# Cross-attention and feed-forward in fp32r halves: four stationary buffers for K's two-batch tiles, an earlier x of tile 1, and another order of the setup

## Chip, cores and metric

The kernel runs on one core of a Trainium2 chip. The metric is device time in microseconds, measured over whole executions; one further execution was recorded by the hardware profiler, and all rows of the trace come from it.

## What is computed

Cut to what matters:

```python
xn  = layernorm(x)                                   # (16, 1024, 512), no weights
lat = ln2(xn);  kv = ln1(ctx) @ Wkv                  # ctx (16, 64, 512), 16 heads of 64
q   = (lat @ Wq) * (1 + fside) + fside               # per batch and head
x   = x + softmax(q k^T / 8) v @ Wout
x   = x + tanh(layernorm(x) @ weight @ aux1 @ aux2 + bias)
```

Everything is float32, and products are made of a high part (fp32r) and a low part (the rest): hi x hi, hi x lo and lo x hi.

## The kernel before

x has 128 tiles of 128 rows, eight to a batch. Because the context has only 64 rows a batch, the kernel folds the weights into it: for each batch M = Wq k^T (512 x 1024, heads times context rows) and N = v Wout (1024 x 512). A tile then needs three products: scores x M into two banks, probabilities times N, and the feed-forward product with one weight W3 = weight aux1 aux2. Each of the five engines runs one program: a setup (`setup_*`), the folding of M of batches 0 and 1 (`fold_m_pe`, `m0_act`, `m0_dve`), then `slot_*` for t = 0 to 132. Slot t has the scores of tile t, the probabilities' product of tile t-2 and the feed-forward of tile t-4.

**Setup.** `steps` is one list by hand for SP, ACT, DVE and GpSimd; each engine takes out of it what concerns it, in this order, and waits on semaphores. `pe_steps` is TensorE's. "split" makes the high part (ACT, L393, L389) and the low part (DVE, L450, L445) of a weight chunk; "a12" is the evacuation of the four banks of aux1 aux2 (the mixed weight: M_hi, M_lo, L398 and L456), which w3 reads; "w3" that of W3; "stats" and "norm" are the context's layernorm on DVE; "turn" its transpose; "load" a context load. Chunk i + 5 is loaded by SP (L256) at step "split i", after low part i+1-th is done (`s_slo`), so a late low part holds SP and all that SP issues behind. `kv` steps are K and V^T products, with a store each. Beside kv 29 stands "x0", where x of tiles 0 and 1 is loaded.

**K's tiles.** From slot 2 on M of the batches 2 to 15 is made beside the main work: 128 tiles, each 128 rows of M for two (n < 32) or four batches (n >= 32). Tile n needs a stationary `wst` (both heads of Wq, 128 KB, read from `wst_scratch`, L762) and K split into `k_hi`, `k_lo` (512 columns each; a two-batch tile uses columns 0 to 255 only). `tile_pe` (L796, L797) makes four small matmuls, `tile_evacuate` (L812) copies on ACT, `tile_store` (L818) stores. The places A, B, C, D in a slot hold one tile each in slots 2 to 9. There are two buffers, `wst[n % 2]`: SP issues the load of tile n+2 when tile n+1's matmuls are done, at its place in SP's order (`next_wst`), between p's stores (L960), p's loads (L977) and others. A tile's matmuls also wait for the evacuation of the tile before, and the evacuation of tile n >= 2 waits for the store of tile n-2.

**x of a tile.** `load_xT` (L625) brings x turned into the one buffer `xT`; ACT makes `xT_hi` (L917), GpSimd `xT_lo` (L922), TensorE starts the scores (L160: passes with hi, L165: with lo) on the first and needs the second after eight matmuls. xT of tile 1 is loaded at the end of SP's setup, when the low part of tile 0 is done, and ACT splits it after exp(0) of tile 0. DVE reads the scores (L1205), takes the maximum (L1210), GpSimd subtracts it (L1333), ACT makes exp (L1110), DVE the sums (L1216), GpSimd divides (L1340), SP stores p and loads it again by columns, DVE transposes (L1223), ACT and DVE split it (L1115, L1232). The first scores are written over the buffers from which M of batch 1 is stored, so DVE waits there for these stores.

The area of 16 x 512 columns is used twice: in the setup as ring of stages, context, `ku`; later as `xr`, `S[0]`, `S[1]`, `xT`. `S[1][:, 0:D]` lies on `ctx_in[0]`, which is `ku[0]`.

Of the kernel before, what the change touches and what calls it, by code (L numbers as in the profile page):

```python
# [39 lines left out]
F32 = mybir.dt.float32  # L40
F32R = mybir.dt.float32r
ALU = mybir.AluOpType
# [3 lines left out]
P = 128  # L46
BANK = 512
EPS = 1e-5
B, ROWS, D = 16, 1024, 512
# [11 lines left out]
def build(nc, x, x_turned, ctx_rows, fs_cols, ln1_w, ln1_b, ln2_w, ln2_b, wqT, wkv, wout, ffn_wT, aux1T, aux2,  # L61
# [11 lines left out]
    with ExitStack() as ctx:  # L73
# [3 lines left out]
        def sem(name):  # L77
            return ctx.enter_context(nc.semaphore(name))
# [102 lines left out]
        for g in range(2):  # L181
# [19 lines left out]
                 ("split", 4), ("split", 5), ("split", 6), ("a12", 0), ("a12", 1), ("a12", 2), ("a12", 3),  # L201
                 ("turn", 0), ("load", 3), ("turn", 1), ("load", 4), ("stats", 2), ("norm", 2), ("split", 7), ("w3", 0),
                 ("stats", 3), ("norm", 3), ("turn", 2), ("load", 5), ("split", 8), ("w3", 1), ("split", 9),
                 ("turn", 3), ("load", 6), ("w3", 2), ("w3", 3), ("stats", 4), ("norm", 4)]
# [45 lines left out]
        def setup_sp(sp):  # L250
# [29 lines left out]
            for step, i in steps:  # L280
# [32 lines left out]
                if step == "x0":  # L313
                    sp.wait_ge(s_slo, CHUNKS)
                    load_x(sp, 0, 0)
                    load_x(sp, 1, 1)
            store_bias(12)
# [3 lines left out]
            load_xT(sp, 0)  # L321
            load_v(sp, 0)
            sp.wait_ge(s_wstw, 16 * 16)
            load_wst(sp, 0)
            load_wst(sp, 1)
# [8 lines left out]
            load_xT(sp, 1)  # L334
            load_k(sp, 0)
            store_bias(15)
# [240 lines left out]
        s_xT = sem("s_xT")  # L577
# [12 lines left out]
        s_wst, s_tw_half = two("s_wst"), two("s_tw_half")  # L590
# [32 lines left out]
        def load_xT(sp, u):  # L623
            at_least(sp, s_xTl, u)
            sp.dma_start(xT, xT_t[bass.ds(u, 1), :, :].rearrange("o p c -> (o p) c")).then_inc(s_xT, 16)  # L625
# [132 lines left out]

        def load_wst(sp, n):
            if n < TILES:  # L760
                at_least(sp, s_mt, n - 1)
                sp.dma_start(wst[n % 2][:].bitcast(F32).rearrange("p (h d) -> p h d", h=2), wst_scratch[n % 32]).then_inc(s_wst[n % 2], 16)  # L762
# [25 lines left out]
        def tile_pe(pe, n):  # L788
            nb, ps, _ = tile_bufs(n)
            pe.wait_ge(s_wst[n % 2], 16 * (n // 2) + 16)  # L790
            pe.wait_ge(s_kl, n // 4 + 1)
            at_least(pe, s_tev, n)
            for h in range(2):
                own = slice(h * nb * CTX, (h + 1) * nb * CTX)
                st = wst[n % 2][:, h * P:(h + 1) * P]
                pe.matmul(ps[:, own], st, k_hi[:, own], start=True, stop=False)  # L796
                mm = pe.matmul(ps[:, own], st, k_lo[:, own], start=False, stop=True)  # L797
            mm.then_inc(s_mt, 1)
# [113 lines left out]
        def xT_split_hi(act, u):  # L912
            act.wait_ge(s_xT, 16 * u + 16)
            if u == 0:
                act.wait_ge(s_kb, 2 * PAIRS)
            at_least(act, s_sc[1], u)
            act.copy(xT_hi[:], xT).then_inc(s_xTh, 1)  # L917

        def xT_split_lo(eng, u):
            eng.wait_ge(s_xTh, u + 1)  # L920
            at_least(eng, s_sc[1], u)
            eng.tensor_tensor(xT_lo[:], xT, xT_hi[:].bitcast(F32), ALU.subtract).then_inc(s_xTl, 1)  # L922
# [26 lines left out]
        def slot_sp(sp, t, m):  # L949
# [4 lines left out]
            def next_wst(place, u=t):  # L954
                if (u, place) in tile_at:
                    load_wst(sp, tile_at[u, place] + 2)
# [145 lines left out]
        def slot_act(act, t, m):  # L1102
# [60 lines left out]
            if t < 2:  # L1163
                ln1_stats(act, t + 1, t + 1)
            if t < T:
                exp(0)
            if t < 2:
                xT_split_hi(act, t + 1)
# [293 lines left out]
```

## Time and profile before

| | us |
|---|---|
| runs: 2064.44, 2066.11, 2069.52; median | 2066.11 |
| profiled execution, its own time | 2073.66 |
| its span | 2071.4 |
| TensorE busy | 2039.1 |
| DVE, GpSimd, ACT busy | 1515.3, 1341.8, 1319.1 |

The span is what the trace covers; the execution's time has 2.3 us around it. In a timeline row stand start, duration, engine, line, operation, output <- inputs, shapes and count; in brackets how long the engine was idle before it and who released it. SPq is the queue of SyncE, which issues the DMAs. In a row of stretches stand the stretch, its length, and each engine's busy us; then PEclk, TensorE's granted clock (1.00 is 2.4 GHz, 0.50 is 1.2 GHz; between them the stretch holds both), the busy share of the DMA engines and GB/s.

### The profile page before, as it was taken

Reading aid. Unit: us, or ns where it says so; the run is one execution under the profiler, and the core shown is the slowest. Engines: PE = TensorE matmul, PEld = TensorE weight load, DVE = VectorE, ACT = ScalarE, POOL = GpSimd, SP = SyncE. Lnnn points to the kernel's source line nnn. Section 1 sums busy time; section 2 is a strip of 40 time slices with the busy share of each in tenths; the row PEclk is TensorE's granted clock in tenths of the full one; section 3 lists DMA queues with packets and bytes.
Section 4 is the critical chain, followed back from the end, with each engine's and each line's share of the span. In section 5 each row is a group of like instructions: output and inputs, shape, how many; then the busy total and the mean of one; then the engine's idle time right before and its main releaser. Section 6 shows DMA issues by size and latency. Waiting matters only on the chain.

```text
span 2071.4 us, 31429 instructions
## 1 busy us (share of the span) xinstructions
PE 2039.1 (98%) x9232; PEld 1693.0 (82%) x9232; DVE 1515.3 (73%) x2384; ACT 1319.1 (64%) x3005; POOL 1341.8 (65%) x1463
## 2 busy tenths in 40 slices
PE   7998999999999999999999999999999999999998
PEld 6777878888888888888888888888888888888887
DVE  7566667677777777777777777777777777777776
ACT  5455566666766666666666666666666666666654
POOL 2035666766677676767677776767767676767564
PEclk9999999999999999999999999999999999999999
DMA  7556887879888787878778686878766675766653
GB/s 249 180 171 194 236 250 215 248 219 252 236 218 226 208 226 203 228 198 222 216 213 237 195 238 196 227 204 221 220 185 196 181 209 168 208 179 192 182 169 120
DMA packets 502490, 431.55 MB, mean 208 GB/s; under 512 B 54832, under 2 KB 408240, under 8 KB 502320
## 3 DMA queue, kind: packets, MB, share of 16 engines
q1 hardware_dynamic: 502320, 429.54, 74.1%
q8 instruction: 75, 1.23, 0.3%
q14 instruction: 95, 0.78, 0.1%
HBM read 251.33 MB, written 178.06 MB: 207 GB/s over the span
## 4 chain that ended last, share of the span: by engine, by line
PE 91%; DMA 3%; SPq 2%; DVE 1%; ACT 1%; issue 1%; POOL 1%; DVEq 0%; ACTq 0%; POOLq 0%
PE bank L160 37%; PE bank L1069 22%; PE bank L165 18%; PE bank L1072 11%; PE bank L797 1%; PE bank L796 1%; DMA wst<-wst_scratch 1%; DMA kv_scratch<-area 0%; DMA stage_more<-ffn_wT_dram 0%; SPq L305 0%; POOL area L1333 0%; DMA area<-x_turned_dram 0%; DMA m_scratch<-evac 0%; DMA area<-ctx_rows_dram 0%; DMA land<-m_scratch 0%
## 5 line engine op out<-in xcount | busy, mean ns | idle before, releaser
L1333 POOL TENSOR_TENSOR area<-area,row_max 128x256 f32<-128x256 f32 x512 | 354.0, 712 | 159.0 <-DVE row_max L1210 159.0
L160 PE MATMUL bank<-M_hi,xT_hi 128*128 128x512 f32 x1024 | 401.9, 393 | 3.2 <-ACT xT_hi L917 3.2
L160 PE MATMUL bank<-M_lo,xT_hi 128*128 128x512 f32 x1024 | 400.9, 392 | 0.0
L1069 PE MATMUL bank<-N_hi,pT_hi 128*128 128x512 f32 x1024 | 399.5, 390 | 1.0 <-DVE N_lo L887 0.8
L1069 PE MATMUL bank<-N_lo,pT_hi 128*128 128x512 f32 x1024 | 398.5, 389 | 0.0
L1115 ACT CAST pT_hi<-turned 128x512 fp32r<-128x512 f32 x256 | 159.1, 621 | 314.4 <-DVE turned L1223 314.4
L1340 POOL TENSOR_TENSOR area<-area,row_inv 128x512 f32<-128x512 f32 x256 | 268.8, 1050 | 111.3 <-DVE row_inv L1219 111.3
L1357 POOL TENSOR_TENSOR area<-area 128x512 f32<-128x512 f32 x127 | 166.6, 1312 | 236.2 <-ACT area L1154 236.2
L1216 DVE TENSOR_REDUCE row_sum<-area 128x8 f32<-128x512 f32 x256 | 174.3, 681 | 177.4 <-ACT area L1110 177.4
L1232 DVE TENSOR_TENSOR pT_lo<-turned,pT_hi 128x512 fp32r<-128x512 f32 x256 | 198.0, 773 | 125.0 <-ACT pT_hi L1115 124.7
L165 PE MATMUL bank<-M_hi,xT_lo 128*128 128x512 f32 x1024 | 275.5, 391 | 0.2 <-POOL xT_lo L922 0.2
L1072 PE MATMUL bank<-N_hi,pT_lo 128*128 128x512 f32 x1024 | 273.7, 389 | 0.0
L1110 ACT ACTIVATE area<-area 128x512 f32<-128x512 f32 x256 | 160.0, 626 | 137.0 <-POOL area L1333 136.7
L160 PEld LDWEIGHTS bank<-M_hi,xT_hi 128*128 128x128 f32 x1024 | 193.9, 189 | 43.5 <-ACT xT_hi L917 3.1
L165 PEld LDWEIGHTS bank<-M_hi,xT_lo 128*128 128x128 f32 x1024 | 193.4, 189 | 41.1 <-POOL xT_lo L922 0.7
L160 PEld LDWEIGHTS bank<-M_lo,xT_hi 128*128 128x128 f32 x1024 | 193.9, 189 | 39.6
L1069 PEld LDWEIGHTS bank<-N_hi,pT_hi 128*128 128x128 f32 x1024 | 192.3, 188 | 40.6 <-DVE N_lo L887 0.9
L1072 PEld LDWEIGHTS bank<-N_hi,pT_lo 128*128 128x128 f32 x1024 | 192.2, 188 | 40.0
L1069 PEld LDWEIGHTS bank<-N_lo,pT_hi 128*128 128x128 f32 x1024 | 192.3, 188 | 39.3
L1205 DVE SCALAR_TENSOR_TENSOR area<-bank,rs,area 128x512 f32<-128x512 f32 x256 | 187.6, 733 | 30.4 <-PE bank L165 26.6
L160 PE MATMUL bank<-W_hi,x2T_hi 128*128 128x512 f32 (+1 forms) x512 | 199.3, 390 | 0.0
L160 PE MATMUL bank<-W_lo,x2T_hi 128*128 128x512 f32 (+1 forms) x512 | 199.3, 390 | 0.0
(171 smaller groups left out, 3938.3 us busy)
## 6 DMA issues: line engine op xcount, KB each, us to landing
p_scratch<-area SPq DMA_DIRECT2D x256, 256.0 KB, 2.6
p_moved<-p_scratch SPq DMA_DIRECT2D x512, 128.0 KB, 4.2
area<-x_dram SPq DMA_DIRECT2D x128, 256.0 KB, 4.5
area<-x_turned_dram SPq DMA_DIRECT2D x128, 256.0 KB, 4.1
x_scratch<-area SPq DMA_DIRECT2D x127, 256.0 KB, 3.0
x_moved<-x_scratch SPq DMA_DIRECT2D x508, 64.0 KB, 3.5
y_dram<-area SPq DMA_DIRECT2D x127, 256.0 KB, 3.6
land<-m_scratch SPq DMA_DIRECT2D x120, 256.0 KB, 2.8
```

Source lines behind the costliest of these rows:

```text
L160: mm = eng.matmul(ps, sh, mv, start=(n == 0), stop=False)
L165: mm = eng.matmul(ps, sl, mh, start=False, stop=(k == len(pairs) - 1))
L1069: pe.matmul(O_ps[:], st(pT_hi, k), n_cols(mv, k), start=(k == 0 and mv is N_hi), stop=False)
L1072: mm = pe.matmul(O_ps[:], st(pT_lo, k), n_cols(N_hi, k), start=False, stop=(k == 7))
L1110: act.activation(s, s, ACT.Exp).then_inc(s_ex[q], 1)
L1115: act.copy(half_of(pT_hi, q), turned[:]).then_inc(s_pTh[q], 1)
L1205: dve.scalar_tensor_tensor(out=half_of(S[t % 2], q), in0=S_ps[q][:], scalar=rs1[:, 0:1], in1=half_of(bias, q), op0=ALU.mult, op1=ALU.add). ...
L1216: dve.tensor_reduce(row_sum[t % 2][:, hs], heads(half_of(S[t % 2], q)), AX_XY, ALU.add).then_inc(s_sum[q], 1)
L1232: dve.tensor_tensor(half_of(pT_lo, q), turned[:], half_of(pT_hi, q).bitcast(F32), ALU.subtract).then_inc(s_pTl[q], 1)
L1333: last = pool.tensor_tensor(s, s, row.to_broadcast([P, 2, 4, J2]), ALU.subtract)
L1340: pool.tensor_tensor(s, s, inv, ALU.mult).then_inc(s_p[q], 1)
L1357: pool.tensor_tensor(xr[u % RING], xr[u % RING], hid, ALU.add).then_inc(s_y, 1)
```

## The change

Three edits. In the setup, split 6 goes behind the four a12 evacuations, and w3 1 behind turn 3 and load 6. For tile 1, x is loaded right behind tile 0's into `S[1][:, 0:D]`, with a semaphore of its own, waiting for the 15th `ku` low part, and ACT splits it before exp(0) of slot 0 (for tile 2 the split stays after exp(0)); xT of tile 2 then no longer waits for tile 1's low part. For n < 32 there are four stationary buffers, the two new ones in columns 256 to 511 of `k_hi` and `k_lo`: the loads 0 and 1 are issued in "x0", 2 and 3 at the end of the setup, and at the place of tile n stands the load of n+4, which needs tile n's matmuls only.

```diff
--- before.py
+++ after.py
@@ -198,10 +198,10 @@
 
 
         steps = [("split", 0), ("split", 1), ("split", 2), ("stats", 0), ("split", 3), ("norm", 0), ("stats", 1), ("norm", 1),
-                 ("split", 4), ("split", 5), ("split", 6), ("a12", 0), ("a12", 1), ("a12", 2), ("a12", 3),
-                 ("turn", 0), ("load", 3), ("turn", 1), ("load", 4), ("stats", 2), ("norm", 2), ("split", 7), ("w3", 0),
-                 ("stats", 3), ("norm", 3), ("turn", 2), ("load", 5), ("split", 8), ("w3", 1), ("split", 9),
-                 ("turn", 3), ("load", 6), ("w3", 2), ("w3", 3), ("stats", 4), ("norm", 4)]
+                 ("split", 4), ("split", 5), ("a12", 0), ("a12", 1), ("a12", 2), ("a12", 3),
+                 ("split", 6), ("turn", 0), ("load", 3), ("turn", 1), ("load", 4), ("stats", 2), ("norm", 2), ("split", 7), ("w3", 0),
+                 ("stats", 3), ("norm", 3), ("turn", 2), ("load", 5), ("split", 8), ("split", 9),
+                 ("turn", 3), ("load", 6), ("w3", 1), ("w3", 2), ("w3", 3), ("stats", 4), ("norm", 4)]
         beside = {0: [("split", 10), ("stats", 5), ("norm", 5)], 1: [("split", 11), ("load", 7), ("stats", 6), ("norm", 6)],
                   2: [("turn", 4), ("stats", 7), ("norm", 7)], 3: [("split", 12)], 4: [("turn", 5)],
                   5: [("turn", 6), ("split", 13)], 6: [("turn", 7)],
@@ -314,15 +314,16 @@
                     sp.wait_ge(s_slo, CHUNKS)
                     load_x(sp, 0, 0)
                     load_x(sp, 1, 1)
+                    sp.wait_ge(s_wstw, 16 * 16)
+                    load_wst(sp, 0)
+                    load_wst(sp, 1)
             store_bias(12)
             for q in s_kvst:
                 sp.wait_ge(q, 16 * 16)
             load_bias(sp, 0)
             load_xT(sp, 0)
+            load_xT(sp, 1)
             load_v(sp, 0)
-            sp.wait_ge(s_wstw, 16 * 16)
-            load_wst(sp, 0)
-            load_wst(sp, 1)
             for k in range(8):
                 dc, g = m_where(2 * k)
                 for w in s_m1r:
@@ -331,8 +332,9 @@
                 if k in (2, 4):
                     store_bias(12 + k // 2)
             sp.wait_ge(s_m, 16)
-            load_xT(sp, 1)
             load_k(sp, 0)
+            load_wst(sp, 2)
+            load_wst(sp, 3)
             store_bias(15)
 
         def setup_pool(pool):
@@ -574,7 +576,7 @@
         s_xsum1, s_mean1, s_sq1, s_var1, s_rs1 = (sem(n) for n in ("s_xsum1", "s_mean1", "s_sq1", "s_var1", "s_rs1"))
         s_xsum2, s_mean2, s_sq2, s_var2, s_rs2 = (sem(n) for n in ("s_xsum2", "s_mean2", "s_sq2", "s_var2", "s_rs2"))
         s_x2w, s_x2r, s_x2t = sem("s_x2w"), sem("s_x2r"), sem("s_x2t")
-        s_xT = sem("s_xT")
+        s_xT, s_xT1 = sem("s_xT"), sem("s_xT1")
         s_xTh, s_xTl = sem("s_xTh"), sem("s_xTl")
         s_x2Th, s_x2Tl = sem("s_x2Th"), sem("s_x2Tl")
         s_sc, s_sb, s_mx, s_sub, s_ex = two("s_sc"), two("s_sb"), two("s_mx"), two("s_sub"), two("s_ex")
@@ -587,7 +589,7 @@
         s_m1r = two("s_m1r")
         s_m1w = sem("s_m1w")
         s_k0in, s_kz, s_k0h, s_k0l, s_wstw = (sem(n) for n in ("s_k0in", "s_kz", "s_k0h", "s_k0l", "s_wstw"))
-        s_wst, s_tw_half = two("s_wst"), two("s_tw_half")
+        s_wst, s_tw_half = [sem(f"s_wst{i}") for i in range(4)], two("s_tw_half")
         s_mt, s_tev, s_tw = sem("s_mt"), sem("s_tev"), sem("s_tw")
         s_land, s_lh, s_ll = sem("s_land"), sem("s_lh"), sem("s_ll")
         s_n, s_nh, s_nl = sem("s_n"), sem("s_nh"), sem("s_nl")
@@ -621,8 +623,14 @@
             sp.dma_start(xr[r], x_t[bass.ds(u, 1), :, :].rearrange("o p d -> (o p) d")).then_inc(s_xin[r], 16)
 
         def load_xT(sp, u):
-            at_least(sp, s_xTl, u)
-            sp.dma_start(xT, xT_t[bass.ds(u, 1), :, :].rearrange("o p c -> (o p) c")).then_inc(s_xT, 16)
+            if u == 1:
+                sp.wait_ge(s_kul, 2 * PAIRS - 1)
+            else:
+                at_least(sp, s_xTl, u if u > 2 else u - 1)
+            sp.dma_start(xT_in(u), xT_t[bass.ds(u, 1), :, :].rearrange("o p c -> (o p) c")).then_inc(s_xT1 if u == 1 else s_xT, 16)
+
+        def xT_in(u):
+            return S[1][:, 0:D] if u == 1 else xT
 
         def load_bias(sp, b):
             at_least(sp, s_sb[1], 8 * b)
@@ -756,10 +764,17 @@
         def first_of_pair(t):
             return [tile_at[t, place] // 4 for place in "AC" if tile_at.get((t, place), 1) % 4 == 0]
 
+        wst_bufs = [wst[0][:], wst[1][:], k_hi[:, 2 * P:4 * P], k_lo[:, 2 * P:4 * P]]
+
+        def wst_at(n):
+
+            return (n % 4, n // 4) if n < 32 else (n % 2, 8 + (n - 32) // 2)
+
         def load_wst(sp, n):
             if n < TILES:
-                at_least(sp, s_mt, n - 1)
-                sp.dma_start(wst[n % 2][:].bitcast(F32).rearrange("p (h d) -> p h d", h=2), wst_scratch[n % 32]).then_inc(s_wst[n % 2], 16)
+                at_least(sp, s_mt, n - 3 if n < 34 else n - 1)
+                i, _ = wst_at(n)
+                sp.dma_start(wst_bufs[i].bitcast(F32).rearrange("p (h d) -> p h d", h=2), wst_scratch[n % 32]).then_inc(s_wst[i], 16)
 
         def load_k(sp, kp):
             if kp < TILES // 4:
@@ -787,12 +802,13 @@
 
         def tile_pe(pe, n):
             nb, ps, _ = tile_bufs(n)
-            pe.wait_ge(s_wst[n % 2], 16 * (n // 2) + 16)
+            i, before = wst_at(n)
+            pe.wait_ge(s_wst[i], 16 * before + 16)
             pe.wait_ge(s_kl, n // 4 + 1)
             at_least(pe, s_tev, n)
             for h in range(2):
                 own = slice(h * nb * CTX, (h + 1) * nb * CTX)
-                st = wst[n % 2][:, h * P:(h + 1) * P]
+                st = wst_bufs[i][:, h * P:(h + 1) * P]
                 pe.matmul(ps[:, own], st, k_hi[:, own], start=True, stop=False)
                 mm = pe.matmul(ps[:, own], st, k_lo[:, own], start=False, stop=True)
             mm.then_inc(s_mt, 1)
@@ -910,16 +926,19 @@
             pool.tensor_tensor(rs1[:], var1[:], minus_half[:], ALU.pow).then_inc(s_rs1, 1)
 
         def xT_split_hi(act, u):
-            act.wait_ge(s_xT, 16 * u + 16)
+            if u == 1:
+                act.wait_ge(s_xT1, 16)
+            else:
+                act.wait_ge(s_xT, 16 * u if u else 16)
             if u == 0:
                 act.wait_ge(s_kb, 2 * PAIRS)
             at_least(act, s_sc[1], u)
-            act.copy(xT_hi[:], xT).then_inc(s_xTh, 1)
+            act.copy(xT_hi[:], xT_in(u)).then_inc(s_xTh, 1)
 
         def xT_split_lo(eng, u):
             eng.wait_ge(s_xTh, u + 1)
             at_least(eng, s_sc[1], u)
-            eng.tensor_tensor(xT_lo[:], xT, xT_hi[:].bitcast(F32), ALU.subtract).then_inc(s_xTl, 1)
+            eng.tensor_tensor(xT_lo[:], xT_in(u), xT_hi[:].bitcast(F32), ALU.subtract).then_inc(s_xTl, 1)
 
 
         LAST = T - 1
@@ -953,7 +972,11 @@
 
             def next_wst(place, u=t):
                 if (u, place) in tile_at:
-                    load_wst(sp, tile_at[u, place] + 2)
+                    n = tile_at[u, place]
+                    if n < 30:
+                        load_wst(sp, n + 4)
+                    elif n >= 32:
+                        load_wst(sp, n + 2)
 
             def write_p(q):
                 sp.wait_ge(s_p[q], t + 1)
@@ -1162,10 +1185,13 @@
                 v_prepare_act(act, 0)
             if t < 2:
                 ln1_stats(act, t + 1, t + 1)
+            if t == 0:
+                xT_split_hi(act, 1)
             if t < T:
                 exp(0)
+            if t == 1:
+                xT_split_hi(act, 2)
             if t < 2:
-                xT_split_hi(act, t + 1)
                 fold_n_act(act, 0, (range(3), range(3, 5))[t])
             elif t > 2:
                 evacuate("A")
```

## Rows read from the trace of the kernel before

**Rows 1.** The page: engines' busy time; x_turned loads, last figure us to landing.

```profile
PE 2039.1 (98%) x9232; PEld 1693.0 (82%) x9232; DVE 1515.3 (73%) x2384; ACT 1319.1 (64%) x3005; POOL 1341.8 (65%) x1463
...
area<-x_turned_dram SPq DMA_DIRECT2D x128, 256.0 KB, 4.1
```

**Rows 2.** Stretches: us, busy us of PE, PEld, DVE, ACT, POOL; PEclk; DMA share, GB/s.

```profile
192.10:198.30 6.20, 6.20 (x17) 5.04 (x18) 1.63 (x3) 1.71 (x4) 0.73 (x1) 0.50 0.95 251
...
210.40:215.30 4.90, 4.83 (x17) 3.90 (x18) 2.21 (x4) 3.98 (x11) 0.74 (x1) 0.67 0.90 270
...
600.00:2000.00 1400.00, 1400.00 (x6288) 1163.23 (x6287) 1055.05 (x1653) 916.97 (x2111) 978.04 (x1064) 1.00 0.75 206
```

**Rows 3.** The waits of PE: us in total, times, longest us.

```profile
PE bank L796 <- DMA wst<-wst_scratch: 7.0, 5, 2.8
...
PE bank L160 <- DVE M_lo L456: 4.0, 1, 4.0
...
PE bank L160 <- ACT xT_hi L917: 3.2, 2, 2.7
```

**Rows 4.** Timeline of DVE and SP in the setup (start, us, idle before); context landings.

```profile
21.00 1.22 DVE L450 TENSOR_TENSOR Wo_lo<-area,Wo_hi 128x1024 fp32r<-128x1024 f32 x1
...
22.13 2.48 DVE L456 TENSOR_TENSOR M_lo<-bank,M_hi 128x512 fp32r<-128x512 f32 x4
...
22.62 0.91 SPq L262 DMA_DIRECT2D area<-ctx_rows_dram  x2
...
30.42 0.68 DVE L423 BATCH_NORM_STATS2 area<-area 128x6 f32<-128x512 f32 x1
...
38.92 0.69 DVE L456 TENSOR_TENSOR W_lo<-bank,W_hi 128x512 fp32r<-128x512 f32 x1 [0.83 <-ACT W_hi L398]
...
DMA to landing us min/median/max: 4.5/5.7/9.1
```

**Rows 5.** Chain that ended last (start, us), then SP's timeline, before the first scores.

```profile
147.11 5.97 DMA area<-x_turned_dram
...
148.05 1.05 SPq L762 DMA_DIRECT2D wst<-wst_scratch  x2
```

**Rows 6.** Timeline from the first scores: DVE, POOL, PE.

```profile
160.37 0.75 DVE L1205 SCALAR_TENSOR_TENSOR area<-bank,rs,area 128x512 f32<-128x512 f32 x1 [2.00 <-DMA m_scratch<-area]
...
161.92 1.19 POOL L1333 TENSOR_TENSOR area<-area,row_max 128x256 f32<-128x256 f32 x2 [6.84 <-DVE row_max L1210]
...
164.36 1.28 POOL L922 TENSOR_TENSOR xT_lo<-area,xT_hi 128x512 fp32r<-128x512 f32 x1 [1.25 <-ACT xT_hi L917]
...
164.33 0.80 PE L160 MATMUL bank<-M_hi,xT_hi 128*128 128x512 f32 x1 [2.70 <-ACT xT_hi L917]
...
167.83 1.09 PE L165 MATMUL bank<-M_hi,xT_lo 128*128 128x512 f32 x4
```

**Rows 7.** Timeline of tile 0's turned probabilities: DVE, then PE.

```profile
178.48 0.71 DVE L1223 STREAM_TRANSPOSE turned<-p_moved 128x512 f32<-128x512 f32 x1
...
179.75 0.75 DVE L1205 SCALAR_TENSOR_TENSOR area<-bank,rs,area 128x512 f32<-128x512 f32 x1 [0.55 <-PE bank L165]
...
181.56 0.90 DVE L1232 TENSOR_TENSOR pT_lo<-turned,pT_hi 128x512 fp32r<-128x512 f32 x1 [0.34 <-ACT pT_hi L1115]
...
185.84 0.50 PE L1069 MATMUL bank<-N_hi,pT_hi 128*128 128x512 f32 x1 [0.76 <-DVE N_lo L887]
```

**Rows 8.** Timeline of ACT and PE at the tiles; landings of two evac stores (last figure).

```profile
190.60 0.37 ACT L812 COPY evac<-bank 128x256 f32<-128x256 f32 x1 [2.35 <-DMA m_scratch<-evac]
...
192.07 0.47 PE L796 MATMUL bank<-k_hi,wst 128*128 128x128 f32 x1 [2.82 <-DMA wst<-wst_scratch]
...
210.47 0.33 PE L796 MATMUL bank<-k_hi,wst 128*128 128x128 f32 x1 [2.48 <-DMA wst<-wst_scratch]
...
m_scratch<-evac SPq DMA_DIRECT2D x1, 128.0 KB, 3.0
...
m_scratch<-evac SPq DMA_DIRECT2D x1, 128.0 KB, 4.7
```

## Prediction

> **What bounds the kernel now.** I read the page first: the reader is to see TensorE busy 98% of the span [rows 1]. Then the table of stretches: from 600 to 2000 us it is busy 1400.00 of 1400.00 us at clock 1.00 [rows 2]. So nothing there can give time, and every wait that can be removed lies before 320 us. Third, the list of what TensorE waited for [rows 3]: wst loads 7.0 us in five waits, low parts of the mixed weight (M_lo, L456) 4.0, xT_hi 3.2 in two (one of them 2.7). Last, the stretches right behind the long waits [rows 2]: TensorE runs part of them at 1.2 GHz (clock 0.50) instead of 2.4. The loss is length times (1 - clock): 6.2 x 0.50 = 3.1 behind the one of 2.82, 4.9 x 0.33 = 1.6 behind the one of 2.48; behind the wait of 2.70 it is the 3.50 us from 164.33 to 167.83 [rows 6] against 1.8 at full speed, 1.7.
>
> **Part 1, order of the setup.** Today the last a12 low part ends at about 24.6: in front of the four (2.48 us) DVE does the low part of split 6, from 21.00 to 22.13 [rows 4]. With split 6 behind them DVE starts them at 21.00, ends at 23.5, and TensorE's w3 starts 1.1 us sooner. The wait of 4.0 becomes 2.9 us, more than the 2.48 behind which the clock fell, so the slow stretch stays. Little of this arrives. The context tiles go DVE-bound to turn 7, DVE is full up to its wait of 0.83 before the last w3 low part at 38.92 [rows 4], and that wait is all that it can give; w3 1, moved behind turn 3, only keeps turn 3's low part from being late for the first kv product. Against it stands SP: chunk 11 is loaded at "split 6" and waits for the seventh low part, now 24.6 instead of 22.2, and the context loads 3 and 4 are queued behind, issued at 22.62 today and at 25.1 then. With 5.7 us to landing, the median [rows 4], tile 3 comes at 30.8, where DVE wants it at 30.42: 0.3 us back. I carry 0.5 us; bounds 0 and 1.1. From kv 8 on TensorE sets the pace to 153 us and the 0.5 stays.
>
> **Part 2, SP before the first scores.** The first two wst loads cost SP 1.05 us [rows 5]. They move from behind xT(0) into the step "x0", ahead of two kv stores, the bias stores, the bias load and xT(0), in a stretch where SP issues without a pause. So xT(0) is issued 1.05 us later, less the 0.5: 0.55 late. It took 5.97 us to land (from 147.11 to 153.08), against a median of 4.1 for this transfer [rows 1, 5]; with fewer small pieces behind it, it may come up to 1.9 us sooner, or not at all sooner. I take none, since xT(1), of the same size as both wst loads, takes their place. ACT stands at xT_hi(0) with the last evacuations of M of batch 1 queued behind it, and the stores of these release DVE's first scores at 160.37 [rows 6], so that start moves to 160.9. In ends: 1.1 + 1.9 - 1.05 = 1.95 us earlier, or 1.05 later.
>
> **Part 3, x of tile 1.** TensorE comes to tile 1 at 161.63 and waits 2.70 [rows 6]. In the new kernel x is there and ACT makes xT_hi(1) before exp(0), at about 160.5. But GpSimd makes xT_lo(1) behind its two subtractions: 161.92 + 0.55 + 1.2 = 163.7, and 1.28 more is 165.0 [rows 6]. TensorE needs it 1.8 us into the tile, at about 164.0: a new wait of 1.0 where 2.7 and the slow clock were. The third pass starts at 165.0 instead of 167.83, 2.8 us earlier. Most of it is waited away again. The way of tile 0's probabilities (store, load, turn) starts from DVE's first scores, not from TensorE. What it gains is the 1.25 us that GpSimd waited for xT_hi before xT_lo [rows 6], less 0.55, and DVE's three N_lo eat half: 0.3 us at the turn of 178.48 [rows 7]. From there to the second turn, 4.0 us on, DVE waited 0.55 for TensorE's scores and 0.34 for pT_hi [rows 7]; both waits go, so the second turn comes 0.3 + 0.55 + 0.34 = 1.2 us earlier. xT(2), released one step sooner, is hidden: its cover is exp(0) of tile 1, behind which ACT makes it at about 171.6, some 1.4 us after TensorE could take it. If that cover were gone 1.4 us would go too, but only to wait at the N_lo gate (185.84 today).
>
> **Part 4, the wst buffers.** With four buffers tile 3's weight is loaded in the setup, so the wait of 2.82 at 192.07 goes. Next late is what ends it at ACT: TensorE's tile 3 waits for tile 2's evacuation, and that waited for tile 0's store until 190.60, lasting 0.37 [rows 8]. The store (issued 3.0 us before) is behind the p loads on SP, which wait for the second turn. All that is 1.2 earlier, so the evacuation ends at 190.97 - 1.2 = 189.8: the gain is 192.07 - 189.8 = 2.3 us, and TensorE stands about 2.2 us, from 187.6 (185.84 - 1.5 and the 3.3 us of its work from there). That is under 2.48, so I let the clock stay up: 3.1 more. At 210.47 the wait of 2.48 shrinks to one evacuation, 0.37 and two hand-overs, about 0.45: 2.0, and its slow stretch goes: 1.6. The other three wst waits are 7.0 - 2.82 - 2.48 = 1.7 [rows 3, 8]. Issue cost on SP in the slots is the same, one wst load at each place. From tile 32 on two buffers alternate as before: nothing.
>
> **Sum.** 2.3 + 3.1 + 2.0 + 1.6 + 1.7 = 10.7 us. Parts 1 to 3 are inside the 2.3, since the gates in a row only let the last one through. The profiled execution took 2073.66 us (span 2071.4), which gives 2063.0; it is 7.6 over the median of the runs, 2066.11. Carried over to the median: 2066.1 - 10.7 = **2055.4 us**.
>
> A price with a wide bound is that of tile 0's store: 3.0 us to land here [rows 8]; the farthest row, the evacuation's store issued near 269 us, has 4.7 [rows 8]. Then the stand of TensorE is 3.9 us and the clock falls: 2.3 - 1.7 + 0 + 2.0 + 1.6 + 1.7 = 5.9. It is nearest to the row of the same slot, so I take 3.0.
>
> **The rule that speaks against it.** In the rows the waits of 2.48, 2.70 and 2.82 us were followed by matmuls at 1.2 GHz, the wait of 0.76 was not [rows 2, 6, 7], and nothing lies between. My sum has TensorE stand 1.5, 1.0, 1.4, 1.5 and 2.2 us in the 35 us from 153 to 189, just in that gap. The Trainium skill, "TensorE: Matmul & The Clock Gate", section "A second HAM failure mode: psum-queue depth-cycling", says that frequent short idles between groups of matmuls make the clock swing too. By that rule the time would be that of rival (a) or (c). No row here shows a stand of 1 to 2.4 us, so whether the trace agrees is open.
>
> **Rivals.** (a) *Many short stands, a low clock behind each.* Five of them at 1.7 us (behind 2.70) take 8.5 off: 10.7 - 8.5 = 2.2, so 2063.9. For it: five stands close together. Against: 0.8 did nothing. 0.12. (b) *The store takes the load's place*, with its landing at 4.7 as above: gain 5.9, 2060.2. For: ACT already waited 2.35 us for that store [rows 8]. Against: fewer loads are under way there. 0.19. (c) *Slower*: the place is the same five stands; if each costs 3.1 us, as behind 192.07, they take 15.5 and the kernel ends 4.8 slower, 2070.9. It decides from 10.7 / 5 = 2.1 us a stand on. Of the three measured only one is over that. 0.03, some of it over the bound for slower. (d) *The change does not do what it says*: SP reaches the loads late all the same, because it is held by p's stores, and only the 1.7 and the 2.3 come: 4.0, 2062.1. Against: the loads of tiles 2 and 3 stand in the setup, before any store of p. 0.04.
>
> **How the numbers follow.** The forecast has 0.62. Its own range is 9 to 13 us of gain: the first scores' start may be 2.5 us earlier than taken (1.95 + 0.55), and one slow stretch kept takes 1.7. A measurement of this kernel tells 0.3% from no change, 6.2 us. Faster by more: all of the forecast and of (b), which lies at the bound, a good half and of (d) a little: 0.74. Within: (a) and the rest: 0.23. Slower: 0.03. For 8 in 10 the range must take in (b) and the good end with 2 us of scatter between runs: 2050 to 2062.5.
>
> **What would show it.** Right: no TensorE wait on wst in the list; the M_lo wait at 2.9; waits on xT_lo, xT_hi, N_lo and the evacuation of 1 to 2 us each between 153 and 190; clock 1.00 from 168 on; all starts after 320 us earlier by about 11. Wrong: slow clock behind those waits; the evacuation wait over 2.48; or xT_hi(0) over 2 us late.

## The result: 5.6 us sooner, where 10.7 were forecast

| | before | changed |
|---|---|---|
| median of 9 runs each, us | 2067.43 | 2061.85 |
| lowest, highest | 2063.59, 2070.06 | 2058.58, 2067.94 |
| profiled execution, its span | 2073.66, 2071.4 | 2061.87, 2059.7 |

The ratio is 0.9974, with a 95% interval from 0.9962 to 0.9986: 5.6 us less, just inside the 6.2 us that were called no change. The forecast's 2055.4 is some 6 us too fast, and its range up to 2062.5 holds the time. The two profiled executions alone differ by 11.8 us, which looks like the forecast. The one of before isn't among the nine runs, and is slower than all of them. That it isn't typical is half of this case.

The page of the changed kernel, engines' busy time, answers to [rows 1]:

```profile
span 2059.7 us, 31428 instructions
...
PE 2031.9 (99%) x9232; PEld 1687.4 (82%) x9232; DVE 1515.1 (74%) x2384; ACT 1318.5 (64%) x3005; POOL 1343.5 (65%) x1463
```

The waits of PE in the changed kernel (us in total, times, longest), against [rows 3]:

```profile
PE bank L812 <- ACT evac L828: 4.4, 3, 2.0
PE bank L160 <- DVE N_lo L458: 2.2, 1, 2.2
PE bank L160 <- DVE M_lo L458: 2.1, 1, 2.1
PE bank L160 <- ACT xT_hi L936: 1.9, 2, 1.1
PE bank L165 <- POOL xT_lo L941: 1.0, 1, 1.0
PE bank L546 <- DVE area L438: 0.9, 1, 0.9
```

No wait for wst is left. In the place of its 7.0 us stand 4.4 us for ACT's evacuation; the M_lo wait is 2.1 where it was 4.0. TensorE's timeline shows where the new stands are (in brackets how long it stood, and who released it):

```profile
23.45 0.47 PE L160 MATMUL bank<-M_hi 128*128 128x512 f32 x1 [2.11 <-DVE M_lo L458]
...
152.23 0.47 PE L160 MATMUL bank<-M_hi,xT_hi 128*128 128x512 f32 x1 [1.10 <-ACT xT_hi L936]
...
163.04 1.20 PE L165 MATMUL bank<-M_hi,xT_lo 128*128 128x512 f32 x4 [1.05 <-POOL xT_lo L941]
...
169.83 0.50 PE L160 MATMUL bank<-M_hi,xT_hi 128*128 128x512 f32 x1 [0.82 <-ACT xT_hi L936]
...
181.81 0.50 PE L1092 MATMUL bank<-N_hi,pT_hi 128*128 128x512 f32 x1 [0.76 <-DVE N_lo L903]
...
187.20 0.30 PE L812 MATMUL bank<-k_hi,k_lo 128*128 128x128 f32 x1 [1.97 <-ACT evac L828]
...
200.94 0.30 PE L812 MATMUL bank<-k_hi,k_lo 128*128 128x128 f32 x1 [0.84 <-ACT evac L828]
...
273.60 0.30 PE L812 MATMUL bank<-k_hi,wst 128*128 128x128 f32 x1 [1.57 <-ACT evac L828]
```

Tile 3 starts at 187.20, where it was 192.07 [rows 8], and tile 7 at 200.94, where it was 210.47. The stretches of the changed kernel behind the stand of 1.97, and in the steady part:

```profile
187.00:193.00 6.00, 5.80 (x28) 4.92 (x29) 3.53 (x5) 2.40 (x6) 1.53 (x3) 1.00 0.96 285
...
600.00:2000.00 1400.00, 1400.00 (x6287) 1163.08 (x6286) 1055.79 (x1654) 915.64 (x2107) 979.58 (x1065) 1.00 0.74 206
```

The clock is 1.00 in both, where the first was 0.50 behind 192.07 [rows 2]. The steady part is as before. Nearly all that differs lies ahead of 320 us; between 340 and 600 TensorE is idle 0.83 us, where it was 0.25. One slow stretch is left in the changed kernel, in the setup behind the N_lo stand of 2.18 at 62.90; the row gives its clock as 0.67:

```profile
62.00:66.00 4.00, 3.10 (x8) 2.48 (x9) 3.78 (x8) 0.70 (x2) 0.00 (x0) 0.67 0.41 156
```

### The profile page after: what moved, and what is told of

Its sections match the earlier page's. It is cut to its first block, busy times and chain, and to the rows that moved or that the text cites. A ratio compares the mean times of both kernels' runs of the same rounds, so it can differ in the third digit from the quotient of the medians.

```text
span 2059.7 us, 31428 instructions
## 1 busy us (share of the span) xinstructions
PE 2031.9 (99%) x9232; PEld 1687.4 (82%) x9232; DVE 1515.1 (74%) x2384; ACT 1318.5 (64%) x3005; POOL 1343.5 (65%) x1463
## 4 chain that ended last, share of the span: by engine, by line
PE 83%; DMA 2%; issue 2%; ACT 2%; DVE 2%; POOL 1%; SPq 1%; DVEq 0%; ACTq 0%; POOLq 0%
PE bank L160 33%; PE bank L1092 21%; PE bank L165 17%; PE bank L1095 10%; DMA m_scratch<-evac 2%; PE bank L813 1%; PE bank L812 1%; POOL area L1359 1%; POOL area L1366 1%; DVE area L1231 0%; DVE N_lo L903 0%; DVE row_max L1236 0%; ACT evac L828 0%; ACT bank L908 0%; DMA area<-x_turned_dram 0%
## 5 line engine op out<-in xcount | busy, mean ns | idle before, releaser
L1138 ACT CAST pT_hi<-turned 128x512 fp32r<-128x512 f32 x256 | 159.1, 622 | 317.4 <-DVE turned L1249 317.4
```

The costliest lines, as they stand in the source:

```text
L1138: act.copy(half_of(pT_hi, q), turned[:]).then_inc(s_pTh[q], 1)
```

## The experiments

Two theories were set against each other. *Profile:* the single profile of before held stands and slow stretches of its own, and terms were sized on these. *New waits:* the expected gain arrives, and waits that come in its place eat it. The first eight kernels ran in two groups of four, the last three together; each group was timed beside the kernel before, whose medians were 2067.17, 2067.73 and 2068.21.

**The kernel before once more** (no edit).

> The kernel before, unchanged, once more with a profile of its own. The changed kernel's profiled span is 11.7 us shorter than that of before (2059.7 against 2071.4), but its median only 5.6 us lower. Theory A: the profiled execution of before lies at the slow end of its own spread, because TensorE's clock fell to 1.2 GHz behind more of its waits than in most executions; then most executions here have a mean clock of 0.996 to 0.998 instead of 0.994, a span of 2062 to 2068, and the new profile shows full clock behind at least one of the waits of 2.4 to 2.8 us, with the waits themselves within 0.5 us. Theory B: the waits themselves differ from run to run, through the landings of the transfers; then the clock stays at 0.994 and the waits of 2.8 (wst), 2.7 (xT_hi) and 4.0 (M_lo) differ by over 1 us in sum. Ratio 1.000 either way.

2067.31 us, ratio 1.0002 (0.9992 to 1.0011), profiled span 2068.8, clock 0.995. Its waits of PE, then two rows of its timeline:

```profile
PE bank L160 <- DVE M_lo L456: 4.1, 1, 4.1
...
PE bank L160 <- ACT xT_hi L917: 3.9, 2, 3.4
...
PE bank L796 <- DMA wst<-wst_scratch: 3.3, 2, 2.7
```

```profile
208.16 0.30 PE L796 MATMUL bank<-k_hi,wst 128*128 128x128 f32 x1 [0.55 <-DMA wst<-wst_scratch]
...
281.86 0.30 PE L796 MATMUL bank<-k_hi,wst 128*128 128x128 f32 x1 [2.53 <-ACT evac L812]
```

The wst waits are 3.3 us in two, not 7.0 in five. Tile 7 stands 0.55 where [rows 8] had 2.48, with nothing slow behind it, and at 281.86 us there is a stand of 2.53, while the profile of before has four of 0.18 to 0.86 between 274 and 305 us. The stands of 4.0, 2.70 and 2.82 are there again (4.14, 3.42, 2.75), each with its slow clock. What made tile 7's stand is one landing of its weight, the step that ended last there, in the profile of before and then in this one:

```profile
205.66 4.77 DMA wst<-wst_scratch
```

```profile
205.28 2.76 DMA wst<-wst_scratch
```

With the setup alone the same load took 2.79 us, and the median of this transfer in the profile of before is 2.7. So this stand came of the landing, as the expectation's second theory says. Its first, full clock behind a wait of nearly the same length, is seen too, at the N_lo wait near 64 us: 2.40 us with 1.2 GHz behind it in the profile of before, 1.91 with clock 1.00 behind it here.

**The setup's order alone.** The diff is the first hunk, with nothing else changed.

> Only the order of the setup (split 6 behind a12, w3 1 behind turn 3). Theory of the prediction: w3 starts 1.1 us sooner, kv 8 only 0.5 us sooner, the rest as before: 0.5 us. Rival from the changed kernel's trace, where the wait on M_lo is 2.1 us and the clock stays up behind it: 2 us less at w3 0 and about 1.5 us at kv 8 (62.9 instead of 64.3), and this stays to the end: 1 to 2 us.

2066.53 us, 0.9996 (0.9988 to 1.0005). The M_lo stand is 3.41, and then the clock falls; DVE's first scores start at 159.1, and tile 3 comes 31.7 us behind them, as before (192.07 - 160.37).

**x of tile 1 alone** (xT(1) into `S[1][:, 0:D]`, with its semaphore and place, and the split ahead of exp(0)).

> Only x of tile 1 (loaded behind that of tile 0 into S[1], split before exp(0)). Theory of the prediction: tile 1 starts without a wait on xT_hi, waits 1 us for xT_lo, the clock stays up, and most is waited away again at the N_lo gate and at wst of tile 3, whose load stands behind p's store: 0 to 2 us at the end. Rival: the 2.8 us gained at tile 1 and its clock come through: 3 us or more.

2067.43 us, 0.9997 (0.9988 to 1.0006). The stand of 2.70 is gone, and tile 3 stands 2.65 for wst, slow clock behind it. Yet in this profile tile 3 starts 28.8 us behind DVE's first scores, where it was 31.7, so part of the gain comes through that gate. Behind it 1.2 GHz follows three stands (2.65, 1.47, 1.80). The median shows no gain; where it is lost, one profile doesn't show.

**The wst buffers alone** (`wst_bufs`, `wst_at`, the loads and their waits).

> Only the four wst buffers and their loads. Theory of the prediction: the waits of 2.8 and 2.5 us on wst become waits on the evacuation of about 2 and 0.5 us, the first loads cost SP 1.05 us before xT(0), and the gain is 6 to 9 us against the profiled execution of before, half of it slow clock. Rival: in a median execution that slow clock is mostly absent, or the evacuation wait is as long as the load's was: 2 to 4 us.

2064.01 us, 0.9982 (0.9973 to 0.9991): of the three parts alone the only one whose interval lies under 1. TensorE's timeline at tile 3, then the stretch behind it:

```profile
188.16 0.30 PE L806 MATMUL bank<-k_hi,k_lo 128*128 128x128 f32 x1 [1.81 <-ACT evac L822]
```

```profile
188.00:194.00 6.00, 5.83 (x21) 4.74 (x22) 2.85 (x4) 2.35 (x6) 0.73 (x1) 0.72 0.95 271
```

The evacuation's stand, 1.81 us where 2.2 were forecast, is followed by 1.2 GHz here: 6.0 x 0.28 = 1.7 us. The gain of 3.2 us in the median is what the expectation gave its rival, 2 to 4 us.

**The changed kernel once more** (no edit).

> The changed kernel once more, unchanged, with a profile of its own. Theory (the clock is a draw): before, 33 runs had a mean clock of 0.9965, the changed one 0.9983 in 9. Each stand of 1.8 to 2.2 us is followed by 1.2 GHz in some executions and not in others (1.97 us without in the changed kernel's profile, 1.81 and 1.93 us with it in the one with the wst buffers alone). Then the clock of 11 more runs is spread over 0.996 to 0.999, the median is 2061 to 2063, and the profile shows the same stands within 0.5 us but another set of slow stretches, each costing about 1.7 us or a multiple. Rival: the clock is a property of the kernel, 0.998 or 0.999 in all runs, and the profile repeats the one slow stretch, at the stand of 2.2 us near 63.

2062.68 us, 0.9972 (0.9958 to 0.9985), clock 0.998. Its timeline at tile 3 and the stretch behind:

```profile
189.19 0.30 PE L812 MATMUL bank<-k_hi,k_lo 128*128 128x128 f32 x1 [1.85 <-ACT evac L828]
```

```profile
189.00:195.00 6.00, 5.81 (x21) 4.72 (x22) 2.85 (x4) 2.38 (x6) 0.74 (x1) 0.72 0.95 268
```

The same kernel, the same stand within 0.12 us, and this time the clock falls. What that costs can be read directly, from tile 3's start to the first matmul of the next tile, in the first profile and in this one:

```profile
193.18 0.22 PE L812 MATMUL bank<-k_hi,wst 128*128 128x128 f32 x1
```

```profile
196.79 0.22 PE L812 MATMUL bank<-k_hi,wst 128*128 128x128 f32 x1
```

193.18 - 187.20 = 5.98 us and 196.79 - 189.19 = 7.60 us: 1.6 us, near the 1.7 by the clock. Not all of it stays. Tile 7 then stands 0.55 and not 0.84, and from tile 3's start to tile 7's the difference is 1.3 us (15.07 against 13.74). DVE's first scores start at 160.9, in the other profile at 159.0.

**A third evacuation buffer**, in the raw K's unused half, for the tiles 0 to 26, so that no evacuation waits for the store of two tiles before.

```diff
+            if nb == 2:
+                return nb, tile_ps[:, at:at + nb * P], (evac[:, 0:2 * P], evac[:, 2 * P:4 * P], k_raw[:, 2 * P:4 * P])[evac_at(n)[0]]
             return nb, tile_ps[:, at:at + nb * P], evac[:, at:at + nb * P]
+
+        def evac_at(n):
+            return (n % 3, n // 3) if n < 27 else ((n - 27) % 2, 9 + (n - 27) // 2)
...
-                at_least(act, s_tw_half[n % 2], 16 * (n // 2))
+                at_least(act, s_tw_half[evac_at(n)[0]], 16 * evac_at(n)[1])
```

> The changed kernel with a third buffer for the evacuated two-batch tiles, in the half of k_raw that they leave free, so that tile n's evacuation waits for the store of tile n-3 and not n-2 (tiles 0 to 26). Theory (the store took the load's place): the stand of 1.97 us at tile 3 shrinks to about 0.5, the one of 0.84 at tile 7 to about 0.45, and the kernel is 1.5 to 2 us faster, more where the clock fell behind that stand. The stand of 1.57 near 274, where ACT is held by the landing of a part of M and not by a store, stays. Rival: the tile waits for something else next, p or k_lo, and nothing is gained.

2060.89 us, 0.9967 (0.9957 to 0.9977). TensorE's timeline at tile 3:

```profile
185.03 0.30 PE L822 MATMUL bank<-k_hi,k_lo 128*128 128x128 f32 x1 [0.55 <-ACT k_raw L838]
```

The store was the gate: with another buffer the stand is 0.55. But in slot 8 TensorE now stands 2.64 (at 272.29), slow clock behind it. The time isn't told apart from that of the changed kernel.

**The first two wst loads back behind xT(0), xT(1) and v.**

```diff
-                    sp.wait_ge(s_wstw, 16 * 16)
-                    load_wst(sp, 0)
-                    load_wst(sp, 1)
...
             load_v(sp, 0)
+            sp.wait_ge(s_wstw, 16 * 16)
+            load_wst(sp, 0)
+            load_wst(sp, 1)
```

> The changed kernel with the first two wst loads back behind xT(0), xT(1) and v. Theory of the prediction, part 2: xT(0) is issued 1.05 us sooner, the stand before the first scores (1.10 us) falls to about 0.1, the first scores of DVE come up to 1 us sooner, and so does all that follows: 0.5 to 1 us. Rival: xT(0) then lands later, with more small pieces around it, and nothing is gained.

2062.15 us, 0.9974 (0.9965 to 0.9983). Its timeline of PE at tile 1:

```profile
160.63 0.47 PE L160 MATMUL bank<-M_hi,xT_hi 128*128 128x512 f32 x1 [1.13 <-DVE area L1231]
```

The stand for xT_hi(0) is gone, and one of the same length, for DVE's first scores, has its place. But the repeat of the changed kernel has no stand for xT_hi(0) either, so this can't be put down to the edit. DVE's first scores start at 159.7, between the two of the changed kernel. SP issues xT(0) at 145.47, and in the changed kernel's first profile at 145.63: only 0.16 of the 1.05 us show, and the 0.5 to 1 us expected in the time don't come.

**GpSimd makes xT_lo(1) ahead of its first subtraction.**

```diff
+            if t == 0:
+                xT_split_lo(pool, 1)
             if t < T:
                 subtract_maximum(0)
-            if t == 0:
-                xT_split_lo(pool, 1)
```

> The changed kernel with xT_lo(1) ahead of GpSimd's first subtraction in slot 0. Theory of the prediction, part 3: the stand of 1.05 us at tile 1 goes, but the subtraction and all of tile 0's probabilities come up to 1 us later, and since their way sets the later gates (N_lo, the evacuation), the kernel gets no faster or up to 1 us slower. Rival: TensorE's own work sets the pace there and 1 us is gained.

2061.27 us, 0.9974 (0.9964 to 0.9983). Its timeline at tile 2:

```profile
169.37 0.50 PE L160 MATMUL bank<-M_hi,xT_hi 128*128 128x512 f32 x1 [1.80 <-ACT xT_hi L936]
```

The stand of 1.05 is gone and tile 2's is 1.80 instead of 0.82: 1.05 given up, 0.98 taken back. Tile 3's is 1.77, at clock 1.00 behind it.

**The third buffer, and in slot 8 ACT's high part of the landed M behind exp(0) and the evacuation.** The slot's stand is ACT's: in the changed kernel it stood for the landing of a part of M before it came to the evacuation. ACT's timeline there:

```profile
272.04 0.62 ACT L873 CAST M_hi<-land 128x512 fp32r<-128x512 f32 x1 [3.82 <-DMA land<-m_scratch]
...
273.10 0.35 ACT L828 COPY evac<-bank 128x256 f32<-128x256 f32 x1
```

```diff
-            if t > 1 and landed_in(t) is not None:
+            if t > 1 and t != TPB and landed_in(t) is not None:
                 land_hi(act, landed_in(t))
...
                 evacuate("A")
+                if t == TPB:
+                    land_hi(act, t)
```

> The kernel with three evacuation buffers, and in slot 8 ACT takes the landed part of M after exp(0) and the evacuation of place A, not before them. Theory: the stand of 1.57 us (2.64 with three buffers) near 272 is ACT standing 3.8 to 5.3 us at that part's landing with exp(0) and the evacuation queued behind it; with the order turned the evacuation is done 1 to 3 us sooner, the stand falls below 0.6 and the kernel gains 1 to 2 us. Rival: the stand moves to exp(1) and the evacuation of place B, since GpSimd still stands for the same part ahead of its second subtraction, and nothing is gained.

2058.68 us in 5 runs, 0.9947 (0.9935 to 0.9960). ACT's timeline in it:

```profile
268.29 0.63 ACT L1143 ACTIVATE area<-area 128x512 f32<-128x512 f32 x1 [1.52 <-POOL area L1371]
...
268.83 0.35 ACT L838 COPY evac<-bank 128x256 f32<-128x256 f32 x1
...
269.73 0.62 ACT L883 CAST M_hi<-land 128x512 fp32r<-128x512 f32 x1 [0.55 <-DMA land<-m_scratch]
```

The evacuation now comes ahead of the wait, and no stand of TensorE is left in the slots 7 to 9. With 9.5 us under the kernel before (2068.21) it is the fastest version here, on few runs. Its interval ends at 0.9960; those of the changed kernel begin at 0.9962 and, in the repeat, at 0.9958, and that of the third buffer alone at 0.9957.

**The changed kernel without x of tile 1** (the second and third part only).

> The changed kernel without the part on x of tile 1 (order of the setup and wst buffers kept). Alone, that part moved nothing (ratio 0.9997). If the parts add up, this is as fast as the changed kernel, 2062 to 2063. If it only pays where the wst gate behind it is gone, this is 1 to 2 us slower than the changed kernel, 2063 to 2064, with a stand of 1.5 us on xT_hi at tile 1 instead of 1.05 on xT_lo.

2062.71 us, 0.9976 (0.9965 to 0.9987), against 0.9974 and 0.9972 with x. Tile 1 stands 1.99 for xT_hi (the clock stays up), tile 3 1.75.

**The changed kernel without the setup's order.**

> The changed kernel without the new order of the setup. The prediction gave that order 0.5 us; the traces show kv 8 1.4 us sooner (62.9 and 63.2 against 64.3 and 64.7) and no slow clock behind the wait for M_lo, where it cost 1.5 to 2.9 us before. If that arrives at the end, this is 1 to 2 us slower than the changed kernel, 2063 to 2064, with its clock back at 1.2 GHz behind a wait of 4 us near 24. If the prediction's 0.5 us is right, 2062 to 2063.

2063.26 us, 0.9972 (0.9961 to 0.9983). The M_lo stand is 3.83 again, slow clock behind it, and in slot 8 a stand of 2.12 has one too. The time doesn't tell the two apart, though the median is the highest of the variants of the changed kernel.

## Why the prediction was wrong in size

**What failed is the step "Carried over to the median".** The 10.7 us were read from one execution and taken off the median of others. Every run lists its mean granted clock. In 92 runs of the kernel before (11 of the repeat, 81 beside the three groups) it lies between 0.994 and 0.999, on average 0.9963, and the mean time goes with it: 2071.7 us at 0.994, 2068.3 at 0.996, 2065.0 at 0.998. The profile that the sum rests on has 0.994, as only two of the 92 do, and its 2073.66 us lie above all of them (2073.56 at most). The text saw that it was 7.6 us over the median and took the difference for something apart from the sum. It was part of it: terms of the sum were what made this execution slow. The repeat's profile is at the slow end too (0.995, 2070.99 us), so no profile shows a typical execution of the kernel before.

- *The stand at tile 7, 2.0, and its slow stretch, 1.6.* It was 0.55 in the repeat of before and with the setup alone, 1.47 with x alone. The changed kernel has 0.84 and 0.55. So two of the four profiles with the old buffers had nothing to give at this place. The cause is a landing of 4.77 us, where 2.76 and 2.79 were measured in those two. The mean stand is 1.26 us in these four and 0.77 in the seven profiles with the new wst buffers and two evacuation buffers, and 1.2 GHz followed it in two of the four and in none of the seven: some 0.5 and 0.9 us in the place of 2.0 and 1.6. This term is the largest error.
- *Three later wst waits, 1.7.* These go, and near 273 us a stand for the evacuation comes (1.57 and 0.97) that the sum did not have: ACT's 3.82 us for the landed part of M. The slots 7 to 9 give up 1.9 us of small waits and take back 1.0 to 1.6, so 0.3 to 0.9 is left. The repeat of before has a stand of 2.53 for the evacuation at 281.86 already, so such a stand isn't the change's alone.
- *The gate of tile 3, 2.3 plus 3.1 for the clock.* The mechanism held: the evacuation, waiting for tile 0's store, ends next; TensorE stood 1.97 and 1.85 where 2.2 were forecast, and the third buffer removed it (0.55). The store landed in 2.9 us, where 3.0 were taken and rival (b) had 4.7. The clock's 3.1 is only in part there: the stand was followed by clock 1.00 in one profile and by 0.72, 1.7 us, in the other. And a slow stretch isn't worth its full length: tile 7's stand was 0.55 in the three profiles with the clock low behind tile 3's evacuation stand, and 0.84 to 1.01 in the four where it stayed up, so that from tile 3's start to tile 7's they are 15.1 and 13.9 us apart on average, 1.2 us and not 1.7.

In place of the clock terms, 3.1 + 1.6 = 4.7 us: the mean granted clock of 16 runs of the changed kernel is 0.9982, 0.0019 over that of before, which is 0.0019 x 2066 = 3.9 us at face value. Compared at equal clock, 0.998, it is 2061.6 us (9 runs) against 2065.0 (6 runs): 3.4 of the 5.6 us aren't clock, 2.2 are. The clock is listed to 0.001 only, which alone is some 2 us. The two ways leave 2 to 4 us for each, and the runs don't settle it nearer.

The bound by which the text let the clock stay up, a stand under 2.48 us, was not in its trace either. It says that nothing lies between 0.76 and 2.48; the profile of before has the N_lo stand of 2.40 in the setup, with 1.2 GHz in the stretch behind it:

```profile
64.31 0.50 PE L160 MATMUL bank<-N_hi,Wo_hi 128*128 128x512 f32 x1 [2.40 <-DVE N_lo L456]
```

```profile
64.00:70.00 6.00, 5.69 (x18) 4.55 (x19) 5.32 (x11) 0.60 (x2) 0.00 (x0) 0.72 0.22 82
```

**Part 1, half right.** The low part came earlier as said: the stand ends at 23.5 on average with the new order and at 24.7 with the old, 1.2 us where 1.1 were forecast. But it shrank to 1.8 to 2.5 us in seven profiles, not 2.9, and the clock stayed up behind each (the eighth with this order, the setup alone, has 3.41 and the slow clock). In the five with the old order it is 3.8 to 4.6, slow behind each. What shortened it further isn't the low part. The first 24 matmuls, the same work in every version, took 7.9 to 8.3 us in these seven, 6.9 in the setup alone, and 6.9 to 7.4 in four of the five with the old order (7.8 in the wst buffers alone). Rows of TensorE's timeline from the changed kernel and from the setup alone:

```profile
11.25 0.63 PE L526 MATMUL bank<-M_lo,M_hi 128*128 128x512 f32 x1
```

```profile
11.18 0.39 PE L525 MATMUL bank<-M_hi,M_lo 128*128 128x512 f32 x1
```

A matmul of 0.63 us is what stands in the stretches at 1.2 GHz, one of 0.39 in those at 2.4, though the granted clock of the view is 1.00 at both places. So part of the shorter stand, and perhaps the clock that stayed up behind it, came from work that ran longer in front of it. The rest of the setup takes some back: seven of the eight with the new order have a new stand of 0.9 at the context's turn 3, and behind the N_lo stand near 63 us 1.2 GHz follows in all eight with the new order, but in only two of the five with the old. The first kv product waiting for N_lo (62.90) starts on average at 62.9 with the new order and 64.4 with the old, 1.5 us; DVE's first scores start only 0.6 sooner (159.2, mean of eight, against 159.8, mean of five), near the 0.5 carried. What was wrong was "from kv 8 on TensorE sets the pace": from there to the first scores other waits take back the rest.

**Part 2, right that nothing is gained.** The first scores were forecast at 160.9, and stand at 159.0 and 160.9; the loads moved back changed nothing that can be told. The 1.05 us by which xT(0) was to be issued later aren't seen in the first profile: it is issued 82.7 us behind the end of the N_lo stand (145.63 - 62.90), where it was 82.8 (147.11 - 64.31) and is 82.6 with the loads moved back; in the repeat it is 84.4. TensorE stood 1.10 for xT_hi(0) in the first profile, where 1.5 were forecast, and not at all in the repeat.

**Part 3, right in the main.** The stand on xT_lo was forecast as 1.0 and is 1.05 in both profiles. Those behind it were taken too long: 0.82 and 0.79 at tile 2 (forecast 1.4), 0.76 and 0.95 at the N_lo gate (1.5). "Most of it is waited away again" fits x alone (0.9997), the kernel without x (0.9976) and xT_lo first (0.9974): none shows a gain in time from this part. That it is waits that eat it is seen directly only with xT_lo first, 0.98 of 1.05 us.

**Part 4** carries what can be told from no change, alone 0.9982. The parts alone give 0.4, 0.3 and 1.8 permille, 2.5 together, and the whole 2.6: nothing in these shows that one part needs another.

**The rivals.** (a), a low clock behind each of five short stands, didn't come: none of the five was slow in the one profile; of the four in the repeat one was. The Trainium skill, "TensorE: Matmul & The Clock Gate", section "A second HAM failure mode: psum-queue depth-cycling", says that frequent short idles let the clock swing. With stands of 0.8 to 2.0 us this case's traces agree only for those of about 1.5 us and more, and there in some executions. (b) was right in its mechanism, the store takes the load's place, and wrong in its price; its 2060.2 is nearer to the time than the forecast, by way of a landing that didn't happen. (c) and (d) fell: the one slow stretch behind the short stands cost 1.7 us, not 3.1, and the loads were in time, though (d)'s 2062.1 is by number the nearest of all. The case that was left out is the one that came: that the profile itself was unusual. The signs named for "right" couldn't tell it: the changed kernel's first profile has no wst wait, waits of 0.8 to 2.0 us between 153 and 190, clock 1.00 from 168 on, and DVE starts tile 11's scores 12.4 us earlier (318.91 against 331.26).

**Still open.** What decides between two executions with a stand of the same length whether the clock falls. And why TensorE's first matmuls run long in some executions: the thirteen profiles don't tell whether the new order has a part in it. They tell where the stands' gain goes. Over the first 340 us, in 1-us stretches, TensorE's idle time is 26.5 and 26.0 us in the two profiles of before, 21.4 and 21.7 in those of the changed kernel, and 18.7 in the fastest version; the loss at 1.2 GHz (busy time x (1 - clock)) is 9.6 and 9.3, then 1.7 and 3.4, then 1.6. But TensorE's span less both is 2035.3 and 2033.5 in the two profiles of before and 2036.5 and 2036.1 in those of the changed kernel. The 1 to 3 us between them lie mostly in the setup: up to the end of the M_lo stand this rest is 14.6 us on average in the seven profiles with the short stand and 13.7 in the other six, and from there to the end of the N_lo stand 36.2 against 35.6. The first 0.9 us are the first matmuls' slow pace, which the granted clock doesn't show; it shortens the stand behind it and costs no time there: the stand ends at 23.58 in the setup alone, where the first matmuls are fast, and at 23.2 to 24.0 in the seven. The idle time thus overstates what the change gave.

## What to carry to other kernels

Before a term is read off one profile, place that profile among the timed runs, by its time and its mean clock: a stand found in an execution that is 0.3% over the median may be what makes it so, and its length is no expectation. Give such a term half, or bound it by nothing. When a load is given more buffers, look for the next one in the ring behind it: here the evacuation, then the landing that stood in front of the evacuation on ACT. Moving that wait behind the evacuation, together with a third buffer, gave 9.5 us in 5 runs, where the changed kernel gave 5.6 and the third buffer alone 6.8.

## What was not expected of the hardware

The same stand of TensorE has two outcomes. Tile 3's was 1.75 to 1.97 us long in seven profiles. It was followed by clock 1.00 in four (1.97, 1.85, 1.77, 1.75) and by 0.72 over 6 us in three (1.85, 1.81, 1.81). Beside the 1.85 of the repeat, which was slow, here is the 1.85 of the kernel without the setup's order, TensorE's timeline and the stretch behind it:

```profile
188.08 0.30 PE L812 MATMUL bank<-k_hi,k_lo 128*128 128x128 f32 x1 [1.85 <-ACT evac L828]
```

```profile
188.00:194.00 6.00, 5.92 (x28) 5.03 (x29) 3.53 (x5) 2.28 (x5) 1.64 (x3) 1.00 0.91 265
```

And the stretch behind the 1.77 of the kernel with xT_lo first:

```profile
186.00:192.00 6.00, 5.52 (x26) 4.68 (x27) 3.53 (x5) 2.67 (x6) 1.22 (x2) 1.00 0.94 264
```

The DMA share doesn't part them: 0.91 to 0.97 in the four, 0.95 to 0.99 in the three. Between 150 and 290 us all stands over 2.0 us were followed by 1.2 GHz, none under 1.4 was, and between them both happened. In the setup the same lengths count for less at one place: M_lo stands of 1.8 to 2.5 us were never followed by it, but N_lo stands near 63 us, of 1.7 to 2.7, were in ten profiles of thirteen. The loss comes in portions of about 1.7 us (6.0 x 0.28 here), or two of them, as the 3.1 behind 192.07 [rows 2]. This makes most of the spread between runs of one kernel: with identical code the mean clock lies up to 0.005 apart and the time up to 12 us (the two go together with a correlation of -0.79 in the 92 runs), so a change of a quarter of a percent is read from populations, and its terms from several profiles.
